# Expert tiles and shared rows fetched in column quarters and turned in 32x32 blocks on VectorE, with batched one-hots

## Chip, cores and metric

The kernel runs on one NeuronCore of a Trainium2 chip. The metric is the device time of one execution in microseconds (us). Below, PE is TensorE, DVE is VectorE, ACT is ScalarE, POOL is GpSimd, SP is SyncE.

## What is computed

A gated cross-attention block is followed by a gated mixture of experts, all in float32. x is (4, 512, 512), that is 2048 tokens of 512 features, and the context is of the same size.

```python
x = x + tanh(g_xattn) * xattn(layernorm(x), ctx)        # one head of 512, 512 + 512 keys
x = x + tanh(g_ffn) * moe(layernorm(x))

shared = silu(x @ W1s.T) * (x @ W3s.T) @ W2s.T          # hidden width 704
probs = softmax(x @ Wg.T)                               # 16 experts
topk_w, sel = top_k(probs, 4)
h = silu(einsum('td,efd->etf', x, W1)) * einsum('td,efd->etf', x, W3)   # hidden width 352
routed = einsum('etf,edf->td', h * combine.T[:, :, None], W2)
moe = shared + routed
```

## The kernel before

Four blocks follow each other, each with one instruction stream per engine and with semaphores between them; nothing reorders the instructions. Attention ends at about 434 us. The routing block (names with b_) runs to 552 us: PE computes the shared FFN for the first half of the tokens in two batches of 512, while DVE ranks the 16 probabilities of each token, counts the tokens of each expert and lists them. The expert block (c_) runs to 1051 us. The combining block (d_) computes the shared FFN for the second half of the tokens and adds up four expert rows for each token.

**Precision.** Each float32 operand is held as a high part (rounded to fp32r by ACT) and a low part (the difference, by DVE or POOL). Each product is three matmuls (line 86): high by high, low by high, high by low.

**The list.** 2048 tokens x 4 choices are 8192 slots, padded for each expert to tiles of 128. 128 x 64 one-hot rows (`one_hot`: line 1176 for the row in the tile, line 1177 for the tile) are multiplied by 64 matmuls (line 1286) into `slot_tokens`, the token of each slot. What DVE does between the steps of the shared FFN is in the table `work` of the routing block, whose key counts those steps: 6 of up and 4 of down for each batch.

**The expert block.** Here there are 72 tiles; 8 experts have five and 8 have four. A tile is 128 rows of 512 features, gathered by POOL with an indirect DMA into `xg[v]`, one of four buffers (v = t % 4), four tiles ahead. PE turns it with four transposes into PSUM (`c_ps_x`, line 1471), ACT copies the high part (line 1411) and DVE subtracts for the low one (line 1445). Up is 24 groups of three matmuls into `c_ps_u`, then silu on ACT, the product with it on DVE (`hf`, line 1459), three transposes (`c_ps_h`), high and low again, and down with 27 matmuls into `c_ps_y`. PE's order in step t is: turn(t), down(t - 2), turn_h(t - 1), up(t).

POOL's step t waits until tile t is gathered and turned, copies a column of the list, gathers tile t + 4, and at the first tile of an expert also does the weights: it waits for those of the next expert (`w_in`), computes their low part (`split_expert`, line 986, 128 x 3840 and 96 x 512 elements), waits for `y_ready`, and issues four DMAs for the weights of the expert after it (lines 977 and 978, twice 2.1 MB). At the last expert but one it issues the last down weights and `last_xs`, the first rows of the combining block, instead. SP only stores 16 tiles of zeros here. ACT stores each tile's result to DRAM (`y_dram`, 256 KB).

## Time and profile before

| | us |
|---|---|
| runs (three) | 1169.88, 1174.15, 1181.65; median 1174.15 |
| profiled execution | 1170.14, its span 1168.5 |
| PE busy | 1106.2 (95% of the span) |
| PE loading weights | 940.0 (80%) |
| DVE, ACT, POOL busy | 490.0 (42%), 279.6 (24%), 477.5 (41%) |
| mean granted clock of PE | 0.977 of full speed |

The busy time of an engine tells how much of the span it has instructions in execution; PE's matmuls overlap, so that the durations of single matmuls add up to more than the time they cost. In the timeline a row has a start in us from the start of the span, a duration, and the engine, line, operation and tiles (output <- input); in brackets is the idle time of the engine ahead of it and what ended it. "POOL idle L73" is a small instruction that stands where POOL waits for a semaphore. Times to landing run from the issue of a DMA to its last byte.

### The profile page before, as it was taken

The numbers are of one execution on the slowest core, as the hardware profiler recorded it, in microseconds if no ns is written. First come the engines' busy times: TensorE is split into PE (matmuls) and PEld (weight loads), VectorE is DVE, ScalarE is ACT, GpSimd is POOL, SyncE is SP. The second block draws the span as 40 slices with busy tenths as digits, with TensorE's granted clock in tenths as the row PEclk, the third lists the DMA queues.
The fourth block names the chain that finished last, engine by engine and source line by source line (L and its number), as shares of the span: only waits on it lengthen the run. The fifth ranks groups of instructions, "written<-read, shape, count | busy, mean of one in ns | idle before, by whom it ended". The sixth has DMA issues, their size and how long they took to land. (4 is left out here: it accounts for less than half of the span.)

```text
span 1168.5 us, 18611 instructions
## 1 busy us (share of the span) xinstructions
PE 1106.2 (95%) x5666; PEld 940.0 (80%) x5667; DVE 490.0 (42%) x994; ACT 279.6 (24%) x575; POOL 477.5 (41%) x521
## 2 busy tenths in 40 slices
PE   3999999999999959998989999999999999988997
PEld 3888878878878827686879999999999999977775
DVE  2243463445336255996222222222222222225847
ACT  1231131122113002111223333333333333321210
POOL 4720201201100235101665565556656665617763
PEclk9999999999999968899999999999999999998999
DMA  9411320312220528133864666666666666627785
GB/s 348 193 73 73 122 94 1 141 74 72 108 72 0 225 85 297 36 111 96 325 226 162 216 229 229 238 220 222 236 220 229 229 220 229 215 69 237 226 278 162
DMA packets 54209, 199.70 MB, mean 171 GB/s; under 512 B 7009, under 2 KB 7009, under 8 KB 45985
## 3 DMA queue, kind: packets, MB, share of 16 engines
q0 software_dynamic: 21184, 122.44, 30.1%
q1 hardware_dynamic: 22624, 57.98, 13.9%
q10 hardware_dynamic: 10368, 18.88, 4.3%
q8 instruction: 18, 0.29, 0.1%
q14 instruction: 15, 0.11, 0.0%
HBM read 161.51 MB, written 37.75 MB: 171 GB/s over the span
## 5 line engine op out<-in xcount | busy, mean ns | idle before, releaser
L86 PE MATMUL c_ps_u<-expert_hi,xT_hi 128*128 x576 | 192.7, 335 | 2.0 <-DVE xT_lo L1445 1.9
L86 PE MATMUL c_ps_u<-expert_hi,xT_lo 128*128 x576 | 186.0, 323 | 0.0
L86 PE MATMUL c_ps_u<-expert_lo,xT_hi 128*128 x576 | 185.6, 322 | 0.0
L986 POOL TENSOR_TENSOR expert_lo<-expert_raw,expert_hi (+3 forms) x39 | 158.2, 4079 | 19.9 <-issue 14.0
L73 POOL TENSOR_TENSOR idle<-idle 128x1 f32<-128x1 f32 x91 | 17.5, 192 | 232.0 <-PE c_ps_x L1471 141.3
L86 PEld LDWEIGHTS c_ps_u<-expert_hi,xT_hi 128*128 128x128 f32 x576 | 108.8, 189 | 2.9 <-issue 2.9
L86 PEld LDWEIGHTS c_ps_u<-expert_lo,xT_hi 128*128 128x128 f32 x576 | 109.3, 190 | 0.0
L1459 DVE TENSOR_TENSOR hf<-c_ps_u,gate 128x352 f32<-128x352 f32 x72 | 37.8, 525 | 170.3 <-ACT gate L1434 170.3
L86 PEld LDWEIGHTS c_ps_u<-expert_hi,xT_lo 128*128 128x128 f32 x576 | 108.7, 189 | 0.0
L1449 DVE TENSOR_TENSOR hT_lo<-c_ps_h,hT_hi 128x256 fp32r<-128x256 f32 x72 | 30.6, 425 | 181.4 <-ACT hT_hi L1424 181.4
L86 PE MATMUL c_ps_y<-expert_hi,hT_hi 128*128 (+1 forms) x216 | 91.7, 425 | 2.6 <-DVE hT_lo L1450 2.3
L86 PE MATMUL c_ps_y<-expert_hi,hT_lo 128*128 (+1 forms) x216 | 85.8, 397 | 0.0
L86 PE MATMUL c_ps_y<-expert_lo,hT_hi 128*128 (+1 forms) x216 | 85.6, 396 | 0.0
L1362 POOL DMA_INDIRECT xg<-xn_dram,column x72 | 71.4, 992 | 25.2 <-issue 19.9
L1596 POOL DMA_INDIRECT parts<-y_dram,token_slots x64 | 67.4, 1053 | 24.7 <-issue 19.2
L1434 ACT ACTIVATE gate<-c_ps_u 128x352 f32<-128x352 f32 x72 | 33.4, 464 | 181.4 <-PE c_ps_u L86 181.4
L1417 ACT ACTIVATE y<-c_ps_y 128x512 f32<-128x512 f32 x72 | 43.1, 598 | 113.0 <-PE c_ps_y L86 113.0
L417 DVE TENSOR_TENSOR q_lo<-ps_products,q_hi 128x512 fp32r<-128x512 f32 x32 | 22.1, 692 | 110.5 <-ACT q_hi L349 110.5
L292 POOL TENSOR_TENSOR ln_rstd<-ln_var,minus_half 128x4 f32<-128x4 f32 x8 | 8.2, 1028 | 145.3 <-DVE ln_var L430 145.3
L1623 DVE SCALAR_TENSOR_TENSOR total<-parts,combine_weights,total 128x512 f32<-128x512 f32 x64 | 54.2, 846 | 14.0 <-DMA total<-x_dram 8.3
L1445 DVE TENSOR_TENSOR xT_lo<-c_ps_x,xT_hi 128x512 fp32r<-128x512 f32 x72 | 49.8, 692 | 12.7 <-ACT xT_hi L1411 9.5
L349 ACT ACTIVATE q_hi<-ps_products 128x512 fp32r<-128x512 f32 x32 | 19.2, 598 | 149.4 <-PE ps_products L86 149.4
(268 smaller groups left out, 2454.5 us busy)
## 6 DMA issues: line engine op xcount, KB each, us to landing
expert_hi<-we POOLq DMA_DIRECT2D x16, 1920.0 KB, 7.9
expert_raw<-we POOLq DMA_DIRECT2D x14, 1920.0 KB, 13.0
y_dram<-y ACTq DMA_DIRECT2D x72, 256.0 KB, 2.1
ctxT_hi<-ctxT POOLq DMA_DIRECT2D x4, 1024.0 KB, 7.4
ctxT_raw<-ctxT SPq DMA_DIRECT2D x4, 1024.0 KB, 5.6
ctx_raw<-ctx SPq DMA_DIRECT2D x4, 1024.0 KB, 4.8
r_t<-x SPq DMA_DIRECT2D x4, 1024.0 KB, 5.3
ctx_hi<-ctx POOLq DMA_DIRECT2D x4, 1024.0 KB, 6.9
```

Source lines behind the costliest of these rows:

```text
L86: last = pe.matmul(out, a[i], b[j], start=(n == 0), stop=(n == 3 * len(pairs) - 1))
L349: act.activation(out, ps_m[:, (m.n - 1) % 2, :], ACT.Copy).then_inc(m_hi, 1)
L417: dve.tensor_tensor(lo, ps_m[:, (m.n - 1) % 2, :], hi, ALU.subtract).then_inc(m_free, 1)
L986: last = eng.tensor_tensor(lo, raw, hi, ALU.subtract)
L1362: pool.indirect_dma_start(xg[v][:], None, mem["xn2"], bass.IndirectOffsetOnAxis(ap=at, axis=0)).then_inc(gathered[v], 16)
L1417: act.activation(y[v][:], ps_y[:, v % 2, :], ACT.Copy).then_inc(y_taken, 1)
L1434: act.activation(gate[u][:], ps_u[:, u, 0, 0:FF], ACT.Silu).then_inc(gate_ready, 1)
L1445: dve.tensor_tensor(x[u][1][:], ps_x[:], x[u][0][:], ALU.subtract).then_inc(x_split, 1)
L1449: dve.tensor_tensor(h[u][1][:, 0:2, :], ps_h[:, 0:2, :], h[u][0][:, 0:2, :], ALU.subtract)
L1459: dve.tensor_tensor(hf[u][:], ps_u[:, u, 1, 0:FF], gate[u][:], ALU.mult).then_inc(h_ready, 1)
L1596: pool.indirect_dma_start(parts[v][:, q, :], None, y_d, bass.IndirectOffsetOnAxis(ap=keep["slots"][:, order[c], q:q + 1], axis=0)).then_in ...
L1623: ins = dve.scalar_tensor_tensor(out=total[k][:], in0=parts[c % 4][:, q, :], scalar=keep["weights"][:, order[c], q:q + 1], in1=total[k][:] ...
```

## The change

A tile of an expert no longer reaches PE in its gathered form. `xg[v]` is stored to a DRAM buffer (`bounce`) and loaded back in four DMAs, one for each quarter of the 512 columns, each to its own 32 partitions (`load_sides`); one DVE instruction turns the 32x32 blocks (`turn_sides`) into one buffer `xt`, from which ACT and DVE make the high and low parts. The rows of the up weights are permuted by the host to fit (`sides`). PE's transposes of tiles and `c_ps_x` are gone. The same is done with the rows of the shared FFN in the routing and combining blocks: each load of 128 rows becomes four, and eight times four transposes of PE in each block become eight of DVE. POOL's split of an expert's weights goes in pieces of 512 columns. The first four tiles are gathered by POOL at the routing block's end, and stored and loaded by ACT.

In the routing block the one-hots are built by six large instructions and 16 that multiply by the token (in place of 128 small ones), the counts come one step earlier in `work`, the schedule later, and the 64 matmuls of the list stand before the third up of the second batch instead of the last down. The second expert's weights are asked for when the schedule is made.

```diff
+def bounce(eng, mem, later, v):
+
+    return eng.dma_start(mem["bounce"][v * P:(v + 1) * P], later.xg[v][:])
+
+
+def load_sides(eng, rows, to, sem):
+
+    side = P // SIDE
+    part = rows.rearrange("(g i) (a c) -> a i g c", i=SIDE, a=side)
+    for a in range(side):
+        eng.dma_start(to[a * SIDE:(a + 1) * SIDE, :, :], part[a]).then_inc(sem, 16)
+
+
+def turn_sides(eng, out, rows):
+
+    return eng.transpose(out.rearrange("p k (g i) -> p g k i", i=SIDE), rows[:].rearrange("p g (k j) -> p g k j", j=SIDE))
 
...
+            def turn_about(t, v):
+                sp.wait_ge(x_turned, t - (QUAD - 1))
+                sp.wait_ge(gathered[v], (t + (QUAD - v)) * 4)
+                bounce(sp, mem, later, v).then_inc(bounced[v], 16)
+                sp.wait_ge(bounced[v], (t + (QUAD - v)) * 4)
+                load_sides(sp, mem["bounce"][v * P:(v + 1) * P], later.xs[v], loaded[v])
+
+            with sp.Fori(1, last + 1) as i:
+                for v in range(QUAD):
+                    turn_about(i * QUAD + v, v)
+            turn_about(last * QUAD + QUAD, 0)
...
             def step(t, v):
 
-                pool.wait_ge(gathered[v], (t + (QUAD - v)) * 4)
+                pool.wait_ge(bounced[v], (t + (QUAD - v)) * 4)
                 pool.tensor_copy(column[v][:], keep["index"][:, t + QUAD:t + QUAD + 1] if isinstance(t, int)
-                                 else keep["index"][:, bass.ds(t + QUAD, 1)]).then_inc(column_ready, 1)
-                pool.wait_ge(x_turned, t + 1)
-                pool.wait_ge(column_ready, t + 1)
+                                 else keep["index"][:, bass.ds(t + QUAD, 1)]).then_inc(pool_made, 1)
+                pool.wait_ge(pool_made, t + 2)
                 hold(nc, nc.gpsimd, keep)
                 gather(v, column[v][:])
                 flag = number(pool, t, "turn", 0, 2)
@@ -1382,7 +1440,7 @@
                     base = number(pool, t, "at1", 0, (BUFFERS - 1) * WE)
 
                     pool.wait_ge(w_in, e * 64 + 32)
-                    split_expert(pool, later, base, w_ready)
+                    split_expert(pool, later, base, w_ready, D)
...
-                            pool.dma_start(later.last_xs[i][:], xn2_d[2 * IT + i]).then_inc(keep["last_xs_in"][i], 16)
+                            load_sides(pool, xn2_d[2 * IT + i], later.last_xs[i], keep["last_xs_in"][i])
...
-            def turn(t, u):
+            def turn(t, v):
+                dve.wait_ge(loaded[v], (t + (QUAD - v)) * 16)
+                wait(dve, x_split, t)
+                turn_sides(dve, xt[:], xs[v]).then_inc(x_turned, 1)
+
+            def low(t, u):
                 dve.wait_ge(x_hi, t + 1)
-                dve.tensor_tensor(x[u][1][:], ps_x[:], x[u][0][:], ALU.subtract).then_inc(x_split, 1)
+                dve.tensor_tensor(x[u][1][:], xt[:], x[u][0][:], ALU.subtract).then_inc(x_split, 1)
 
             def turn_h(t, u):
                 dve.wait_ge(h_hi, t + 1)
@@ -1452,25 +1514,20 @@
 
             def step(t, v):
                 u = v % 2
-                turn(t, u)
+                turn(t + 1, (v + 1) % QUAD)
                 if later_than(t, 0):
                     turn_h(t - 1, 1 - u)
+                low(t + 1, 1 - u)
                 dve.wait_ge(gate_ready, t + 1)
                 dve.tensor_tensor(hf[u][:], ps_u[:, u, 1, 0:FF], gate[u][:], ALU.mult).then_inc(h_ready, 1)
 
+            turn(0, 0)
+            low(0, 0)
...
-            def turn(t, v):
-
-                pe.wait_ge(gathered[v], (t + (QUAD - v)) * 4)
-                wait(pe, x_split, t)
-                for k in range(DC):
-                    last = pe.transpose(ps_x[:, k, :], xg[v][:, k * P:(k + 1) * P], keep["ident"][:])
-                last.then_inc(x_turned, 1)
-
             def weights(base, start, n, rows=P):
...
+            def hot_rows(first, n):
+
+                i = slice(first, first + n)
+                dve.tensor_tensor(row_hot[:, i, :], lane[:].unsqueeze(1).broadcast_to([P, n, P]),
+                                  row_no[:, i].unsqueeze(2).broadcast_to([P, n, P]), ALU.is_equal).then_inc(hot_ready, 1)
+
+            def hot_tiles(k):
+
+                hot = tile_hot[k]
+                then(dve.tensor_tensor(hot[:], lane[:, 0:TILES_MAX].unsqueeze(1).broadcast_to([P, HN, TILES_MAX]),
+                                       tile_no[:, k * HN:(k + 1) * HN].unsqueeze(2).broadcast_to([P, HN, TILES_MAX]),
+                                       ALU.is_equal))
+                for j in range(HN // TOPK):
+                    at = k * HN // TOPK + j
+                    last = dve.tensor_scalar(hot[:, j * TOPK:(j + 1) * TOPK, :], hot[:, j * TOPK:(j + 1) * TOPK, :],
+                                             token[:, at:at + 1], None, ALU.mult)
                 last.then_inc(hot_ready, 1)
+
+            def weights():
...
-                    **{at: (lambda j=j: one_hot(j)) for j, at in enumerate(range(10, 17), 1)}}
+            def done():
+                then(dve.tensor_tensor(keep["turn"][:], t_f[:], t_g[:], ALU.mult))
+                dve.memset(t_f[:, 0:1], 0.0).then_inc(scheduled, 1)
+
+            piece = NT * TOPK // PIECES
+            work = {0: lambda: (rank(), choices()), 1: rest_of_down, 2: counts, 3: slots,
+                    4: lambda: hot_rows(0, piece), 5: lambda: hot_rows(piece, piece), 6: lambda: hot_rows(2 * piece, piece),
+                    7: lambda: hot_rows(3 * piece, piece), 8: lambda: hot_tiles(0), 9: lambda: hot_tiles(1),
+                    10: weights, 11: schedule, 13: lambda: places(range(BUFFERS)), 14: lambda: (turns(), done())}
 
             def between(n, k):
                 at = n * (SC + IT) + k
...
 
+                if n * (SC + IT) + j == LIST_AT:
+                    list_slots()
                 if (n, j) != (0, 3):
```

**SP in the expert block.** Before, SP has the stores of zeros and a wait for them. This is what stands behind them now, the first three tiles of its loop over four; `xg_69` to `xg_71` are gathered tiles, `xs_73` to `xs_75` what is loaded back, and `gathered`, `bounced` the semaphores of gather and store.

```order
L1323 DMA bounce_dram<-xg_69 128x512 [waits gathered0]
L1331 DMA xs_73<-bounce_dram 32x4x128 [waits bounced0]
L1331 DMA xs_73<-bounce_dram 32x4x128 x3
L1323 DMA bounce_dram<-xg_70 128x512 [waits gathered1,c_x_turned]
L1331 DMA xs_74<-bounce_dram 32x4x128 [waits bounced1]
L1331 DMA xs_74<-bounce_dram 32x4x128 x3
L1323 DMA bounce_dram<-xg_71 128x512 [waits gathered2,c_x_turned]
L1331 DMA xs_75<-bounce_dram 32x4x128 [waits bounced2]
L1331 DMA xs_75<-bounce_dram 32x4x128 x3
```

Each tile has a store that waits for its gather, and four loads that wait for the store; the next tile's store stands behind them in SP's row.

**POOL at a tile of the expert block, up to the wait ahead of the next weight loads.** Before:

```order
L1373 COPY column_3582<-slot_tokens 128x1 [waits gathered1]
L73 TENSOR_TENSOR idle<-idle 128x1 [waits c_column_ready,c_x_turned]
L1362 DMA xg_70<-xn_dram,column_3582 128x512
L986 TENSOR_TENSOR expert_lo<-expert_raw,expert_hi 128x3840
L986 TENSOR_TENSOR expert_lo<-expert_raw,expert_hi 96x512
L73 TENSOR_TENSOR idle<-idle 128x1 [waits c_y_ready]
```

The same place now:

```order
L1432 COPY column_3514<-slot_tokens 128x1 [waits bounced1]
L74 TENSOR_TENSOR idle<-idle 128x1 [waits c_pool_made]
L1421 DMA xg_70<-xn_dram,column_3514 128x512
L989 TENSOR_TENSOR expert_lo<-expert_raw,expert_hi 128x512
...
L989 TENSOR_TENSOR expert_lo<-expert_raw,expert_hi 128x256
L989 TENSOR_TENSOR expert_lo<-expert_raw,expert_hi 96x512
L74 TENSOR_TENSOR idle<-idle 128x1 [waits c_y_ready]
```

The column copy waits for the store of the tile in place of its gather, the wait for PE's transposes (`c_x_turned`) is gone, and the split is in nine pieces: seven of 512 columns on 128 partitions (the row that is shown, and six like it), one of 256 and one of 512 on 96.

**DVE, two steps of the expert block.** Before:

```order
L1445 TENSOR_TENSOR xT_lo_3566<-c_ps_x,xT_hi_3565 128x512 [waits c_x_hi]
L1449 TENSOR_TENSOR hT_lo_3576<-c_ps_h,hT_hi_3575 128x256 [waits c_h_hi]
L1450 TENSOR_TENSOR hT_lo_3576<-c_ps_h,hT_hi_3575 96x128
L1459 TENSOR_TENSOR hf_3571<-c_ps_u,gate_3569 128x352 [waits c_gate_ready]
L1445 TENSOR_TENSOR xT_lo_3568<-c_ps_x,xT_hi_3567 128x512 [waits c_x_hi]
L1449 TENSOR_TENSOR hT_lo_3574<-c_ps_h,hT_hi_3573 128x256 [waits c_h_hi]
L1450 TENSOR_TENSOR hT_lo_3574<-c_ps_h,hT_hi_3573 96x128
L1459 TENSOR_TENSOR hf_3572<-c_ps_u,gate_3570 128x352 [waits c_gate_ready]
```

Now:

```order
L1336 STREAM_TRANSPOSE xT<-xs_76 128x4x4x32 [waits c_x_split,tile_in3]
L1511 TENSOR_TENSOR hT_lo_3512<-c_ps_h,hT_hi_3511 128x256 [waits c_h_hi]
L1512 TENSOR_TENSOR hT_lo_3512<-c_ps_h,hT_hi_3511 96x128
L1507 TENSOR_TENSOR xT_lo_3500<-xT,xT_hi_3499 128x512 [waits c_x_hi]
L1522 TENSOR_TENSOR hf_3507<-c_ps_u,gate_3505 128x352 [waits c_gate_ready]
L1336 STREAM_TRANSPOSE xT<-xs_73 128x4x4x32 [waits c_x_split,tile_in0]
L1511 TENSOR_TENSOR hT_lo_3510<-c_ps_h,hT_hi_3509 128x256 [waits c_h_hi]
L1512 TENSOR_TENSOR hT_lo_3510<-c_ps_h,hT_hi_3509 96x128
L1507 TENSOR_TENSOR xT_lo_3498<-xT,xT_hi_3497 128x512 [waits c_x_hi]
L1522 TENSOR_TENSOR hf_3508<-c_ps_u,gate_3506 128x352 [waits c_gate_ready]
```

A transpose of the next tile stands at the head of each step, the subtract for the next tile comes behind the low part of h, and it reads `xT` from SBUF where it read `c_ps_x`.

## Rows read from the trace of the kernel before

**Rows 1.** Busy time of each engine, 600 to 1040 us; then clock, DMA share.

```profile
600.00:1040.00 440.00, 440.00 (x2631) 409.53 (x2630) 120.46 (x262) 143.78 (x330) 256.85 (x300) 1.00 0.61 215
```

**Rows 2.** The tile c_ps_x: who waited for it, us and times.

```profile
  POOL idle L73: 141.3, 37
```

**Rows 3.** Timeline of POOL in one expert: start, duration, instruction, [idle before].

```profile
733.69 0.60 POOL L977 DMA_DIRECT2D expert_hi<-we  x1
...
735.38 0.54 POOL L978 DMA_DIRECT2D expert_raw<-we_rest  x1
...
736.96 1.01 POOL L1362 DMA_INDIRECT xg<-xn_dram,column  x1 [0.50 <-issue]
...
755.50 0.98 POOL L1362 DMA_INDIRECT xg<-xn_dram,column  x1
...
757.30 9.73 POOL L986 TENSOR_TENSOR expert_lo<-expert_raw,expert_hi  x2 [0.82 <-issue]
...
767.13 0.60 POOL L977 DMA_DIRECT2D expert_hi<-we  x1
```

**Rows 4.** Timeline of POOL and PE, first three weight loads and a stop.

```profile
575.69 0.59 POOL L977 DMA_DIRECT2D expert_hi<-we  x1
...
591.90 0.78 PE L1471 MATMUL c_ps_x<-ident,xg 128*128 128x128 f32 x4 [4.63 <-DMA xg<-xn_dram,column]
...
604.80 0.60 POOL L977 DMA_DIRECT2D expert_hi<-we  x1
...
639.93 0.60 POOL L977 DMA_DIRECT2D expert_hi<-we  x1
```

**Rows 5.** Timeline of PE at one tile's transposes.

```profile
854.90 0.60 PE L1471 MATMUL c_ps_x<-ident,xg 128*128 128x128 f32 x4
855.26 0.48 PE L86 MATMUL c_ps_y<-expert_hi,hT_hi 128*128 x1
```

**Rows 6.** DMAs issued at 735-738, 725, 436, 1007: KB, us to landing.

```profile
expert_raw<-we_rest POOLq DMA_DIRECT2D x1, 192.0 KB, 13.5
xg<-xn_dram,column POOLq DMA_INDIRECT x1, 12.4
y_dram<-y ACTq DMA_DIRECT2D x1, 256.0 KB, 10.4
...
y_dram<-y ACTq DMA_DIRECT2D x1, 256.0 KB, 2.0
...
first_xs<-xn_dram SPq DMA_DIRECT2D x1, 256.0 KB, 2.7
...
xg<-xn_dram,column POOLq DMA_INDIRECT x1, 9.2
```

**Rows 7.** Timeline of DVE and SP: two subtracts, four DMA issues.

```profile
461.53 1.15 DVE L938 TENSOR_TENSOR b_h_lo<-b_h,b_h_hi 128x512 fp32r<-128x512 f32 x1
...
856.17 0.69 DVE L1445 TENSOR_TENSOR xT_lo<-c_ps_x,xT_hi 128x512 fp32r<-128x512 f32 x1
...
1051.14 1.80 SPq L1560 DMA_DIRECT2D total<-x_dram  x4
```

**Rows 8.** One line each: ns min/median/max, first and last start.

```profile
L986 POOL TENSOR_TENSOR expert_lo<-expert_raw,expert_hi x9: 976/1302/1736, 460.8 to 471.5; 128x512 fp32r<-128x512 f32 x7, 128x256 fp32r<-128x256 f32 x1, 96x512 fp32r<-96x512 f32 x1
...
L1002 POOL TENSOR_TENSOR last_down_lo<-last_down_raw,last_down_hi x5: 1285/1294/1309, 1073.6 to 1078.6; 128x512 fp32r<-128x512 f32 x5
...
L1623 DVE SCALAR_TENSOR_TENSOR total<-parts,combine_weights,total x64: 740/752/6853, 1065.2 to 1161.3; 128x512 f32<-128x512 f32 x64
...
L1177 DVE TENSOR_SCALAR tile_hot<-lane,tile_no,token x64: 315/321/329, 503.5 to 541.4; 128x80 f16<-128x80 f32 x64
```

**Rows 9.** Timeline of POOL and PE at tile 69.

```profile
1006.92 1.02 POOL L1362 DMA_INDIRECT xg<-xn_dram,column  x1 [0.50 <-issue]
...
1022.21 0.60 PE L1471 MATMUL c_ps_x<-ident,xg 128*128 128x128 f32 x4
```

**Rows 10.** Busy time of each engine, 480 to 486 us, columns as before.

```profile
480.00:486.00 6.00, 5.65 (x15) 3.62 (x15) 5.70 (x12) 2.17 (x4) 0.00 (x0) 0.50 0.00 0
```

More of the change, by code:

```diff
@@ L766 @@
 BUFFERS = 3
[L770 to L771 removed]
 HN = NT * TOPK // 2
+PIECES = 4
+LIST_AT = SC + IT + 2
 class Later:
@@ L786, in __init__ @@
         self.xg = [sb(f"xg{v}", [P, D], F32) for v in range(QUAD)]
+        self.xs = [sb(f"xs{v}", [P, P // SIDE, P], F32) for v in range(QUAD)]
         self.behind_xg = sb.at
@@ L795, in __init__ @@
         over = Sbuf(nc, self.second_hi)
-        last = over("first_xs3", [P, D], F32)
-        over.at = first_free + 4 * 4 * DC * D * 2
-        self.first_xs = [over(f"first_xs{i}", [P, D], F32) for i in range(IT - 1)] + [last]
+        sides = [P, P // SIDE, P]
+        last = over("first_xs3", sides, F32)
+        over.at = self.first_xs_at = first_free + 4 * 4 * DC * D * 2
+        self.first_xs = [over(f"first_xs{i}", sides, F32) for i in range(IT - 1)] + [last]
         self.behind_xs = over.at
@@ L809, in __init__ @@
         self.last_d_hi = over("last_down_hi", [P, SC, D], F32R)
-        xs = [over(f"last_xs{i}", [P, D], F32) for i in range(2)]
+        xs = [over(f"last_xs{i}", sides, F32) for i in range(2)]
         assert over.at <= self.second_hi + 4 * WE
@@ L814, in __init__ @@
         self.last_d_raw = low[1]("last_down_raw", [P, SC, D], F32)
-        self.last_xs = xs + [low[0](f"last_xs{i}", [P, D], F32) for i in range(2, 4)]
+        self.last_xs = xs + [low[0](f"last_xs{i}", sides, F32) for i in range(2, 4)]
         assert low[0].at <= self.second_lo + 4 * WE
@@ L882, in down @@
             tripled(pe, self.ps_y[:, i % 2, :], pairs, split).then_inc(self.y_ready, 1)
-        for i in range(IT):
-            turn(0, i)
         up_ready()
@@ L942, in vector @@
             turn(0, i)
+            if i:
+                split(0, i - 1)
+        split(0, IT - 1)
         for n in range(2):
@@ L966, in vector @@
                     turn(1, i + 2)
+                if n == 0 and i < IT - 1:
+                    split(1, i + 1)
                 between(n, SC + i)
@@ L1118, in _ @@
             sh.scalar(act)
+            for v in range(QUAD):
+                act.wait_ge(keep["gathered"][v], 16)
+                bounce(act, mem, later, v).then_inc(keep["bounced"][v], 16)
+            for v in range(QUAD):
+                act.wait_ge(keep["bounced"][v], 16)
+                load_sides(act, mem["bounce"][v * P:(v + 1) * P], later.xs[v], keep["loaded"][v])
         @block.vector
@@ L1154, in count, with choose, slots @@
                 keep["cum"] = cum
[L1156 to L1165 removed]
+            def choose(what, out):
+                for k in range(TOPK):
+                    then(dve.scalar_tensor_tensor(out=f["one"][:], in0=keep["ranks"][:], scalar=float(k),
+                                                  in1=what[:], op0=ALU.is_equal, op1=ALU.mult))
+                    then(dve.tensor_reduce(out[:, :, k], f["one"][:], AX.X, ALU.add))
+            def slots():
+                choose(f["slot"], slot_f)
                 then(dve.tensor_copy(keep["slots"][:], slot_f[:]))
@@ L1297, in expert_phase @@
         sb = Sbuf(nc, later.behind_xg)
-        xg, gathered = later.xg, keep["gathered"]
+        xg, xs = later.xg, later.xs
+        gathered, bounced, loaded = keep["gathered"], keep["bounced"], keep["loaded"]
+        xt = sb("xT", [P, DC, P], F32)
         x = [(sb(f"xT_hi{u}", [P, DC, P], F32R), sb(f"xT_lo{u}", [P, DC, P], F32R)) for u in range(2)]
+        y = [sb(f"y{v}", [P, D], F32) for v in range(QUAD)]
         gate = [sb(f"gate{u}", [P, FF], F32) for u in range(2)]
@@ L1654, in program @@
         keep["up_ready"], keep["first_ready"] = sem("up_ready"), sem("expert_split")
-        keep["first_xs_in"], keep["gathered"] = ([sem(f"{n}{i}") for i in range(4)] for n in ("first_xs_in", "gathered"))
+        keep["first_xs_in"], keep["gathered"], keep["bounced"], keep["loaded"] = (
+            [sem(f"{n}{i}") for i in range(4)] for n in ("first_xs_in", "gathered", "bounced", "tile_in"))
         keep["y_out"], keep["base_out"] = [sem(f"y_out{v}") for v in range(QUAD)], [sem(f"base_out{u}") for u in range(2)]
```

118 lines of the change are left out of this document (48 added, 70 removed).

## Prediction

> **What bounds the kernel now.** I read the busy time by stretch first, then the tiles of the expert block one engine at a time. From 600 to 1040 us PE is busy 440.0 of 440 us at full clock, while DVE and POOL have 27% and 58% of that stretch [rows 1]. What the change takes from PE there counts in full, as long as nothing else paces the tiles. The second reading asks how far off the others are. POOL is not idle for want of work: 141.3 us of its waits end with a c_ps_x transpose [rows 2], so it is held to PE's pace by the very instruction that goes. Its cycle for an expert of five tiles: weights asked for at 733.69, split begun at 757.30, next weights at 767.13 [rows 3]. That is 33.44 us, 6.69 for each tile of PE; an expert of four tiles takes 26.75. In the first expert, where PE was ahead of POOL, the same chain had PE idle for 4.63 us behind a gather [rows 4].
>
> **PE's transposes.** The first transpose of a tile starts at 854.90, the down matmul behind it at 855.26, and takes 0.48 us itself [rows 5]: 0.36, and my allowance of 0.06 for the slower start of another kind of matmul, 0.42 us a tile. The durations of the four overlap and don't add up to what PE gets back. 72 x 0.42 = 30 us if PE stays the bound; a five-tile expert would fall from 33.44 to 31.35 us, a four-tile one from 26.75 to 25.1.
>
> **The new path of a tile.** A tile is now gathered, stored to DRAM by SP, loaded back by four DMAs of SP, and turned on DVE. No row shows a DMA with 512-byte runs or a DVE transpose. For the store: 256 KB from SBUF landed after 2.0 us unloaded, and after 10.4 us when it was issued some 4 us after the weight loads [rows 6]. I take 2.3 where the weights have landed. For the load: 2.7 us for 256 KB in one piece [rows 6], bounds 2 and 5. SP's four loads of the combining block took 1.80 us to issue [rows 7], 0.45 each, so a tile holds SP for 0.15 + 2.3 + 4 x 0.45 = 4.3 us, below the 6.27 us of a tile: SP keeps up on the average. For the DVE transpose I take the 0.69 us that a 128x512 subtract needs [rows 7]; bounds 0.3 and 2. DVE's 27% becomes about 38%, so it is no bound by its busy time.
>
> The Trainium skill (DMA: Bandwidth & Descriptors, Rules for kernel authors) counts transfers under 64 KB as mostly overhead and asks to coalesce; four loads of 64 KB with 512-byte rows stand at its edge. The trace has no such load. By it the upper bound of 5 us would hold, and the sum below would be about 3 us higher in each place where a load is on the path.
>
> **The loop that will pace the experts.** POOL no longer waits for PE's transposes but for the store of the tile (`bounced`). Follow it from the first weight load of an expert, called L. The weights are in 15.2 us later (the last part issued at 735.38, 13.5 to landing); the gather behind them, issued 3.3 us after L, takes 12.4 us and lands at L + 15.7 [rows 3, 6]. In an expert of five tiles just this gather brings the tile at whose step the next split stands. So: 15.7 + 0.1 (wait) + 2.3 (store) + 0.1 + 2.06 (from the end of the last weight issue to that of the gather, 735.92 to 737.97) + 0.85 (from the gather at 755.50 + 0.98 to the split at 757.30, at most) + split + 0.15.
>
> The split was one piece of 3840 columns and one of 512, 9.73 us [rows 3]. It is now eight of 512 and one of 256, at 1.26 us for 512 (five took 6.29 [rows 8]): 8 x 1.26 + 0.65 = 10.7 us. DVE now has a subtract with both inputs in SBUF, turned beside these pieces; where such pieces ran beside such subtracts, in the routing block, a piece took up to 1.74 us and a subtract to 1.15 [rows 7, 8]. Two or three meet in one split: 11.5 us. The loop is 32.8 us, with 32.1 and 34 as its ends. Before: 33.44. **So of PE's 2.1 us a five-tile expert keeps 0.65.** A four-tile expert waits for its weights: 15.2 + 0.1 + 11.5 + 0.15 = 26.95, against 26.75 before: it loses 0.2.
>
> One thing more on SP. The gathers behind the weights land close together, and SP takes them 4.3 us apart. The fourth store is then issued at about L + 15.7 + 3 x 4.3 = L + 28.6. After a four-tile loop that is behind the next weight load, where a store takes 10 us and not 2; half of that is covered by the tiles ready ahead, and I count 1 us for each such loop.
>
> From 604.80 on there are six loops of five tiles and six of four. The first of five took 35.1 us [rows 4], and comes to 32.8 (-2.3); the other five give 5 x -0.65 = -3.2; the four-tile ones 6 x 0.2 = +1.2, and 6 x 1 = +6 for the late stores. Sum: +1.7.
>
> **The first expert.** L is at 575.69; the gather of tile 5 landed only at 591.9, and PE stood 4.63 us for it [rows 4]. Now PE would wait for store, load, transpose, high and low as well: 2.3 + 2.7 + 0.7 + 0.6 + 0.7, and it has 2 us less work in front. Only the tiles' end moves, and part of the next loop's slack takes it up: the next L was at 604.80; by the loop above it is 575.69 + 16.2 (the landing here) + 0.1 + 2.3 + 2.3 + 0.85 + 11.5 + 0.15 = 609.1. **+4.3.**
>
> **The end of the stage.** Behind the DMAs of the last weights and the four of last_xs, POOL issued the gather of tile 69 at 1006.92, with 9.2 us to landing [rows 6, 9]. It now stands behind 12 more issues, at 0.54 each as the one at 735.38 [rows 3] 6.6 us, and has store, load, transpose and split behind it, 7 us, before PE gets it. It landed at 1016.2 and was used at 1022.2 [rows 9], 6 us of slack. 6.6 + 7 - 6 = +7.6, less the part of these issues in which the queue has drained and the gather is quicker, 2 us: **+5**.
>
> **The other blocks.** In the routing block 32 PE transposes go (eight tiles, 8 x 0.4 = -3 us at most; four stand where PE waited anyway). The 128 one-hot instructions (64 of them of 0.32 us [rows 8]) become 4 + 2 large ones and 16 of 320 columns: by 0.69 us for 512 columns, 4 x 2.7 + 2 x 3.4 + 16 x 0.4 = 24 us, against some 27 as they overlap now. The counts move one place earlier; behind them PE stood before 480 us, and from 480 to 486 its clock was at 0.50 [rows 10]. That stall moves rather than goes. The list's 64 matmuls leave the end of the block; the gathers could come 5 us earlier, but they wait for the last up's release, the bounce adds 5 us, and the second expert's weights are asked for later. I take **-1** (bounds -5 and +4). In the combining block DVE does 8 more transposes and PE 32 fewer, and the start, where PE waits for DVE, is 0.7 us longer: **+1**. For the clock, one more stop of PE with such a stretch behind it, 6 us at 0.50 in which some 2 to 3 us of work are lost [rows 10]: **+2**.
>
> **The sum.** +1.7 + 4.3 + 5 - 1 + 1 + 2 = +13 us. The profiled execution took 1170.1 us, 4.0 below the median of the three runs, 1174.15; 1170.1 + 13 = 1183, and 1187 on the median's side. One per cent, 12 us, is about what a measurement of this kernel can tell from no change.
>
> **Rivals.**
> *PE stays the bound (0.15).* It needs a loop of 31.35 us: a gather landing 1 us sooner, a split of 10.7, no wait of DVE. For it: pieces of 512 may never meet a DVE subtract, as DVE has some 4 us of them in each 31. Then 66 x -0.42 = -28, with +5 at the start and +3 at the end: -20, 1154 us. Against: the landing at L + 15.7 is the trace's own, and the split can only grow.
> *It cancels (0.20).* Loops at the lower ends (-1.3 and -0.2 each) and no late stores: -9, start and end +8: 1165 to 1178, no difference to be told.
> *DVE is locked out by the split (0.20), the slower side.* In the combining block one DVE operation with two SBUF inputs stood 6.85 us, through five POOL pieces without a gap [rows 8]. If that is the rule for nine pieces, the subtract of the next tile stands 10.7 us, in front of hf and the transposed h that PE's down waits for. It decides from the point at which the lock lasts over one tile, 6.3 us: 4.4 us lost at each expert. 31.35 + 4.4 = 35.8 against 33.44, 25.1 + 4.4 = 29.5 against 26.75, so 16 x 2.5 = +40, and +7 for the ends: 1170 + 47 + 4 = 1221. Against: in the routing block subtracts got in between pieces after 1.15 us.
>
> The Trainium skill (SBUF — State Buffer, Who interferes with whom) says that GpSimd and a DVE instruction with two SBUF inputs lock each other out for a whole instruction. The 6.85 us row agrees and goes beyond it: five instructions, not one. By the page's rule a wait is at most one piece, 1.3 us, and the forecast stands.
>
> **Chances.** The forecast (+13, own range 1178 to 1200) has 0.45, in which a bit more than half lies over 1% slower. With the rivals: faster 0.18 (the first, and a little of the second), within 1% 0.37, slower 0.45. The range takes half of the first rival and half of the third: 1152 to 1222.
>
> **What the next profile would show.** Right: POOL's wait at the column copy ends with the store and not with PE; L to L is 32 to 34 us for five tiles and about 27 for four; PE idles 1 to 2 us in each expert, in c_ps_u behind DVE; PE's share falls below 92%; the gather of tile 69 is late by over 5 us. Wrong, if PE is busy all of 620 to 1000 (first rival), or if DVE's low stands over 5 us in each split (third). What would spoil it besides: 512-byte loads that take over 6 us, or a DVE transpose above 2 us.

## The result and the profile after

The change makes the kernel slower: 1260.34 us (median of four runs, 1257.52 to 1263.85) against 1175.48 us, a ratio of 1.0722 with a 95% interval of 1.066 to 1.0784. The forecast was 1187. The page of the changed kernel:

```profile
span 1256.4 us, 18614 instructions
PE 1095.5 (87%) x5314; PEld 919.9 (73%) x5315; DVE 544.0 (43%) x979; ACT 277.5 (22%) x576; POOL 516.1 (41%) x638
...
bounce_dram<-xg SPq DMA_DIRECT2D x69, 256.0 KB, 2.5
xs<-bounce_dram SPq DMA_DIRECT2D x276, 64.0 KB
```

PE is busy for 11 us less, in a span that is 88 us longer. The first column of the next table runs from the first to the last tile's h transposes (`c_ps_h`), that is the expert block without its edges; all are us.

| | expert block | before it | after it |
|---|---|---|---|
| before | 482.9 | 561.8 | 123.9 |
| changed | 555.1 | 572.7 | 128.5 |

72 us of the loss are in the expert block, 11 ahead of it, 5 behind it. Busy time of each engine in a stretch of the expert block, with the same columns as [rows 1]:

```profile
620.00:1040.00 420.00, 366.61 (x1984) 331.99 (x1984) 141.75 (x276) 117.72 (x276) 246.94 (x340) 0.94 0.75 261
```

PE, busy 100% of such a stretch before, is now idle for 53 us of 420, at a clock of 0.94. The waits of the block, engine by engine (us in total, times, longest; PE and DVE from 600 to 1110 us, POOL from 600 to 1040 us):

```profile
PE c_ps_y L87 <- DVE hT_lo L1512: 78.8, 16, 14.3
...
DVE xT L1336 <- DMA xs<-bounce_dram: 189.2, 37, 18.7
...
POOL column L1432 <- DMA bounce_dram<-xg: 75.7, 9, 11.9
POOL expert_lo L989 <- DMA expert_raw<-we_rest: 39.4, 6, 7.8
POOL idle L74 <- PE c_ps_y L87: 24.6, 10, 4.9
```

These lines are read as a chain. PE stops 16 times for the low part of h, at least once behind each request for weights; DVE has not made it because the turn of the next tile (the DVE transpose) stands ahead of it in DVE's queue; and the turn waits for the four loads of SP. One expert shows why, in the timelines of SP, POOL, DVE and PE (POOL's gap at 826.69 is what [rows 2] was):

```profile
800.07 0.34 SPq L1323 DMA_DIRECT2D bounce_dram<-xg  x1
802.76 1.73 SPq L1331 DMA_DIRECT2D xs<-bounce_dram  x4
804.65 0.34 SPq L1323 DMA_DIRECT2D bounce_dram<-xg  x1
806.76 1.91 SPq L1331 DMA_DIRECT2D xs<-bounce_dram  x4
823.55 0.34 SPq L1323 DMA_DIRECT2D bounce_dram<-xg  x1
826.55 1.73 SPq L1331 DMA_DIRECT2D xs<-bounce_dram  x4
828.39 0.36 SPq L1323 DMA_DIRECT2D bounce_dram<-xg  x1
...
806.40 0.61 POOL L980 DMA_DIRECT2D expert_hi<-we  x1 [1.17 <-issue]
...
826.69 0.19 POOL L1432 COPY column<-slot_tokens 128x1 int32 x1 [11.09 <-DMA bounce_dram<-xg]
...
829.37 11.66 POOL L989 TENSOR_TENSOR expert_lo<-expert_raw,expert_hi  x9 [0.97 <-issue]
...
843.17 0.61 POOL L980 DMA_DIRECT2D expert_hi<-we  x1 [1.07 <-issue]
...
824.07 0.71 DVE L1336 STREAM_TRANSPOSE xT<-xs 128x512 f32<-128x512 f32 x1 [7.62 <-DMA xs<-bounce_dram]
...
825.42 0.49 PE L87 MATMUL c_ps_y<-expert_hi,hT_hi 128*128 x1 [3.78 <-DVE hT_lo L1512]
```

The weights are asked for at 806.40. SP issues the loads of a tile 0.36 us later, and the turn behind them starts at 824.07, 17.7 us after the weights were asked for. That is when weights land: in the six loops where POOL's split waits for them, it starts 15.2 to 17.3 us after they were asked for. The gather issued at 809.45 took as long:

```profile
xg<-xn_dram,column POOLq DMA_INDIRECT x1, 14.0
```

It lands at 823.5, its store at 826.5, and that tile is turned at 830.16, 24 us after the weights were asked for. For 17 us SP starts on no tile; in the rest of the 36.8 us from one weight load to the next it passes four or five, at 4.0 to 5.9 us each, and the loads of the last one run into the next weights. The other experts are like this one: from SP's last DMA for a tile to its next there are 13 to 18 us at 13 of 14 weight loads, 9.5 at the other, and 14.8 in the median.

### The profile page after: what moved, and what is told of

Same layout as the page of the kernel before. It is cut to its first block and busy times, and to the rows that moved or that the text cites. A ratio compares the mean times of both kernels' runs of the same rounds, so it can differ in the third digit from the quotient of the medians.

```text
span 1256.4 us, 18614 instructions
## 1 busy us (share of the span) xinstructions
PE 1095.5 (87%) x5314; PEld 919.9 (73%) x5315; DVE 544.0 (43%) x979; ACT 277.5 (22%) x576; POOL 516.1 (41%) x638
## 5 line engine op out<-in xcount | busy, mean ns | idle before, releaser
L989 POOL TENSOR_TENSOR expert_lo<-expert_raw,expert_hi (+1 forms) x144 | 182.5, 1302 | 50.7 <-DMA expert_raw<-we_rest 40.8
L87 PE MATMUL c_ps_y<-expert_hi,hT_hi 128*128 (+1 forms) x216 | 95.7, 443 | 82.5 <-DVE hT_lo L1512 82.2
L1336 DVE STREAM_TRANSPOSE xT<-xs 128x512 f32<-128x512 f32 x73 | 51.7, 708 | 196.9 <-DMA xs<-bounce_dram 194.0
L87 PEld LDWEIGHTS c_ps_y<-expert_hi,hT_hi 128*128 128x128 f32 (+1 forms) x216 | 45.2, 209 | 95.9 <-issue 88.4
L87 PEld LDWEIGHTS c_ps_u<-expert_lo,xT_hi 128*128 128x128 f32 x576 | 110.6, 192 | 0.0
L87 PE MATMUL c_ps_y<-expert_lo,hT_hi 128*128 (+1 forms) x216 | 93.0, 431 | 0.0
L87 PE MATMUL c_ps_y<-expert_hi,hT_lo 128*128 (+1 forms) x216 | 92.9, 430 | 0.0
L1467 ACT ACTIVATE xT_hi<-xT 128x512 fp32r<-128x512 f32 x73 | 45.8, 628 | 142.3 <-DVE xT L1336 140.4
L1522 DVE TENSOR_TENSOR hf<-c_ps_u,gate 128x352 f32<-128x352 f32 x72 | 37.6, 522 | 85.9 <-ACT gate L1490 70.7
L74 POOL TENSOR_TENSOR idle<-idle 128x1 f32<-128x1 f32 x91 | 18.7, 206 | 128.1 <-PE ps_products L87 69.3
L1507 DVE TENSOR_TENSOR xT_lo<-xT,xT_hi 128x512 fp32r<-128x512 f32 x73 | 62.6, 858 | 5.8 <-ACT xT_hi L1467 5.7
```

What stands on the lines that cost most here:

```text
L74: return eng.tensor_tensor(idle[:, at:at + 1], idle[:, 4:5], idle[:, 4:5], ALU.add)
L87: last = pe.matmul(out, a[i], b[j], start=(n == 0), stop=(n == 3 * len(pairs) - 1))
L989: last = eng.tensor_tensor(lo, raw, hi, ALU.subtract)
L1336: return eng.transpose(out.rearrange("p k (g i) -> p g k i", i=SIDE), rows[:].rearrange("p g (k j) -> p g k j", j=SIDE))
L1467: act.activation(x[u][0][:], xt[:], ACT.Copy).then_inc(x_hi, 1)
L1507: dve.tensor_tensor(x[u][1][:], xt[:], x[u][0][:], ALU.subtract).then_inc(x_split, 1)
```

## The experiments

"Block" is the first column of the table above. Each time is that of one execution, but for the two at the end that have an interval (medians of ten and of twelve). The kernel before, measured beside these runs, took 1181, 1174, 1176, 1173 and 1174 us. Its executions scatter from 1169.84 to 1181.62 us (23 of them) and those of the changed kernel from 1257.52 to 1263.85 (four), so a difference of some 6 us between two single executions tells nothing.

**The expert block as before, the rest as changed.** PE turns the tiles, nothing is stored and loaded back, the split is in two pieces.

```diff
-  the expert block of the changed kernel; sides(w1), sides(w3)
+  the expert block of the kernel before; chunks(w1), chunks(w3)
```

> The expert block of the kernel before (four transposes of PE per tile, gathers used as they land, weights split in two pieces), with the routing and combining blocks of the changed kernel. If the new path of the expert tiles is the cause, the expert block has its 6.7 us a tile again, PE has one stop of some 5 us in it, and the time is 1180 to 1190 us, the routing and combining blocks keeping their +12. Rival, that the slower routing block also spoils the expert block (later second weights, later first tiles): over 1200 us.

1184.15 us, the block 482.4: the block is where it was before (482.9), so the whole of its loss is in its new path and none comes from a late routing block.

**Small weights.**

```diff
-    load_expert(pool, later.w_hi, ...); load_expert(pool, later.w_raw, ...)
+    pool.dma_start(part(w, P, base, 0, D), io["we"][e, :, 0:D])   # w_hi from the fourth expert on, w_raw from the third
```

> The changed kernel, but from the fourth expert on the weight loads carry 512 of 3840 columns (the split does the same work, on what is there), so that the traffic behind which tiles land is an eighth. The output is then not the reference's. If tiles stand behind the weights' transfer, PE's stops in the expert block go to under 1 us for each expert after the first two, and the time to 1165 to 1190 us. If DVE is locked out by POOL's pieces, or SP's serial store and loads are too slow by themselves, the stops stay and the time is above 1230 us.

1167.13 us, the block 464.5. The busy time of the stretch:

```profile
620.00:1040.00 420.00, 413.73 (x2363) 382.66 (x2361) 166.22 (x327) 139.72 (x329) 258.17 (x399) 1.00 0.66 200
```

With the same stores, loads, turns and POOL pieces, PE is idle for 6 us of 420 at full clock. The stops need the weights' transfer. The block is 18 us shorter than before, and 15 us of what is left are still stops: 9.5 us behind the weights of the third expert, whose high part is loaded whole, and 4.5 us near the block's end. Without any stop it would be near 450 us.

**Half the weights.**

```diff
-    load_expert(pool, later.w_raw, base, io, e, w_in)
+    pool.dma_start(part(later.w_raw, P, base, 0, D), io["we"][e, :, 0:D]) ...
```

> The changed kernel, but the raw part of an expert's weights is loaded only in its first 512 of 3840 columns (2.3 MB an expert in place of 4.2; the split does the same work; the output is not the reference's). The transfer then lasts some 9 us in place of 17. An expert of five tiles has 31 us for 9 + 5 x 4.6 = 32, one of four 25 for 9 + 18 = 27: stops of 1 to 2 us in each, 1180 to 1200 us. If the landing of the gather behind the weights were all, there would be none left (the gather lands 8 us earlier): below 1175 us.

1198.56 us, the block 495.6. A transfer half as long leaves a third of PE's waiting for h (28.4 us of 78.8, in 18 stops of at most 4.1 us); the time is at the upper end of what was expected.

**No store.**

```diff
-    bounce(sp, mem, later, v).then_inc(bounced[v], 16)
-    sp.wait_ge(bounced[v], (t + (QUAD - v)) * 4)
-    load_sides(sp, mem["bounce"][v * P:(v + 1) * P], ...)
+    load_sides(sp, mem["xn2"][v * P:(v + 1) * P], ...)
...
-    pool.wait_ge(bounced[v], (t + (QUAD - v)) * 4)     # POOL's step
+    pool.wait_ge(gathered[v], (t + (QUAD - v)) * 4)
```

> The changed kernel, but from the fifth tile on SP doesn't store the gathered tile; once it has landed, the four loads read fixed rows of the normalized input, and POOL goes on at the gather's landing (the tiles then hold other rows, and the output is not the reference's). A tile holds SP for 2 us in place of 4.6. If the time is 17 us of weights plus the tiles one by one, an expert needs 17 + 5 x 2 = 27 us, below PE's 31, and the stops all but go: 1175 to 1200 us. If the loads caught behind the weights stop PE by themselves, whatever the store, it stays above 1225 us.

1183.9 us, the block 484.8. The busy time of the stretch:

```profile
620.00:1040.00 420.00, 401.13 (x2267) 367.52 (x2266) 159.22 (x315) 134.50 (x315) 283.71 (x393) 0.99 0.76 261
```

PE is idle for 19 us of 420 where it was for 53. With 2 us of SP for a tile in place of 4.6 two thirds of the idle time go. The loads still meet the weights, and stops stay: 33.4 us in 12 of them from 600 to 1110 us, one of 12.2 us behind the weights of the third expert and the others of 0.8 to 3.4 us. So most of the loss takes both, a long transfer and a path of DMAs in series, each of which waits for the landing of the one before. The run doesn't part SP's time from POOL's earlier step, since POOL here goes on at the gather's landing.

**One load, or four of whole rows.** The first run loads a tile with one DMA, the second with four DMAs of 32 whole rows.

```diff
-    load_sides(sp, mem["bounce"][v * P:(v + 1) * P], later.xs[v], loaded[v])
+    sp.dma_start(later.xs[v][:], mem["bounce"][v * P:(v + 1) * P])                      # one load
+    for a in range(4): sp.dma_start(later.xs[v][32 a:32 a + 32], mem["bounce"][...])    # four of whole rows
```

> The changed kernel, but SP loads a tile back with one DMA of 256 KB in rows of 2 KB in place of four of 64 KB in rows of 512 bytes (features are then in the wrong order, and the output is not the reference's). If it is the weights' transfer that holds the tiles, whatever their form, the time stays within 1240 to 1262 us. If the four small loads are the cost (issue time, short rows), it falls below 1215 us.

> The changed kernel, but each of the four loads of a tile takes 32 whole rows of 2 KB in place of 128 pieces of 512 bytes (features in the wrong order, the output not the reference's). One load of 2-KB rows gave 1222 us. If the number of loads and their issue on SP made the 38 us, this run is at 1245 to 1262 us; if the 512-byte pieces made it, at 1215 to 1230 us.

1222.24 us with one (block 522.7), 1260.32 with four (554.5). The first result lay between the two expectations, so that the form of the load is a second cause: 38 us. The second shows which part of the form: 2-KB rows in place of 512-byte pieces gain nothing; what is left is that there are four DMAs and not one, with 1.73 us of issuing and not 0.35. SP's timeline with one load:

```profile
815.57 0.34 SPq L1323 DMA_DIRECT2D bounce_dram<-xg  x1
818.64 0.35 SPq L1408 DMA_DIRECT2D xs<-bounce_dram  x1
819.47 0.33 SPq L1323 DMA_DIRECT2D bounce_dram<-xg  x1
822.47 0.35 SPq L1408 DMA_DIRECT2D xs<-bounce_dram  x1
822.99 0.33 SPq L1323 DMA_DIRECT2D bounce_dram<-xg  x1
```

Here a tile takes 3.5 to 3.9 us in place of 4.0 to 5.9, so that more of them pass before the next weights.

**The raw weights behind one or two gathers.**

```diff
     gather(v, column[v][:])
+    load_raw(t - 1)          # t - 2 in the second run: the raw part of an expert asked for one step later
```

> The changed kernel, but the two weight loads of an expert are parted on POOL's queue: first the high part (2.1 MB), then the next tile's gather, then the raw part. The weights' transfer takes as long as before, but that gather stands behind 2 MB and not 4, and should land 8 to 9 us after the first weight load in place of 17. If it is this gather, with its store and load, that PE waits for, the stops shrink by some 4 us for each expert and the time falls to 1190 to 1225 us. If PE waits for the four loads of the tile before, which SP issued just as the weights started, and these are held until all weights are in, the stops stay: 1240 to 1262 us.

> As the run before, with two gathers between the high and the raw part of the weights, the raw part 3 to 4 us later. By the gather theory 1185 to 1220 us, no worse than with one gather, unless the weights' late landing delays the split: then the experts of four tiles grow to over 30 us, and the time is above the run before by 10 us or more.

1274.62 and 1242.22 us: the first is a clear miss for the gather theory and slower than either expectation had it, the second gains 18 us on the changed kernel, which neither of its expectations had. The DMAs of the first run tell why it lost; the first line is the loads of a tile ahead of the weights, the next two are loads and a gather issued 0.5 to 1.8 us behind the first weight load, the last is the store of the tile that this gather brought:

```profile
xs<-bounce_dram SPq DMA_DIRECT2D x4, 64.0 KB, 2.0
...
xs<-bounce_dram SPq DMA_DIRECT2D x4, 64.0 KB, 11.6
...
xg<-xn_dram,column POOLq DMA_INDIRECT x1, 8.8
...
bounce_dram<-xg SPq DMA_DIRECT2D x1, 256.0 KB, 9.3
```

The gather lands after 8.8 us, as foreseen, and nothing is won, since its store then runs beside the raw weights. The four loads landed after 8.7 to 16.9 us, and the turn needs the last of them. Whatever of a tile's three steps meets the weights takes some 9 us or more; to bring one step forward moved the meeting to the next. Why two gathers ahead of the raw weights did better than one was not looked into.

**Two tiles at a time on SP.**

```diff
+    for v in (v0, v0 + 1): wait for gather v; store v
+    for v in (v0, v0 + 1): wait for store v; four loads of v
```

> The changed kernel, but SP takes tiles in pairs: store, store, then the loads of the first and of the second, so that one store's landing is spent on the other's work. A pair should hold SP for some 6.7 us where two tiles held it for 9. If PE waits because SP can pass a tile only while no weights are in flight, and one at a time, an expert gets 4 to 5 us shorter where it stops now, as with the single load (1222 us): 1205 to 1235 us. If a tile's own latency through store and loads decides, the pair makes it worse: over 1255 us.

1255.14 us, where the account above asked for 1205 to 1235. It lies at the edge of the other branch (over 1255), but is not slower than the changed kernel as that branch had it; PE's waits for h are 78.8 us in both. The pair is quicker where both tiles are there, but not where the second is missing:

```profile
832.88 3.65 SPq L1331 DMA_DIRECT2D xs<-bounce_dram  x8
836.69 23.34 SPq L1323 DMA_DIRECT2D bounce_dram<-xg  x2
860.08 1.92 SPq L1331 DMA_DIRECT2D xs<-bounce_dram  x4
```

The first tile's store is issued at 836.69, the second's 23 us later, when its gather has come out from behind the weights, and the first tile's loads stand behind it. So the edit brought a wait of its own. That reading comes after a miss and no further run tests it; the run does not confirm the account above.

**The split: left out, and in two pieces.** In the first run POOL computes the last 96 x 512 only; in the second the pieces are those of before.

```diff
-    split_expert(pool, later, base, w_ready, D)
+    pool.tensor_tensor(lo, raw, hi, ALU.subtract)       # the last piece only; PE reads w_hi for w_lo
+    split_expert(pool, later, base, w_ready)            # second run: 3840 columns, and 512
```

> The changed kernel, but POOL computes the low part of the last 96 x 512 weights only, 1.3 us in place of 11.7, and PE multiplies by the high part where it took the low one (the output is not the reference's). If the tiles' landing behind the weights paces the block, PE's stops shrink only by what the next weight load comes earlier, and the time is 1235 to 1258 us. If the pieces lock out DVE, or POOL's time in them is what keeps the gathers late, it is below 1200 us.

> The changed kernel with the split in two pieces, 8.5 and 1.3 us, as before, in place of nine. The subtract of a tile, with both inputs in SBUF, then stands up to 8.5 us behind the long piece where it stood under 1.8 behind the short ones, but POOL is done 2 us sooner. If such a lock matters beside PE's long stops, the time is 1265 to 1300 us; if the stops hide it, 1250 to 1262 us.

1248.09 us without the split: DVE's lock by POOL (a DVE instruction that can't go on while POOL's runs) and POOL's time in the pieces together are worth 12 us of the 85. 1279.62 us in two pieces, 19 more than in nine. The subtract of the tile (min, median, max in ns), in the changed kernel and in this run:

```profile
L1507 DVE TENSOR_TENSOR xT_lo<-xT,xT_hi x73: 677/691/1781, 564.1 to 1123.8; 128x512 fp32r<-128x512 f32 x73
```

```profile
L1507 DVE TENSOR_TENSOR xT_lo<-xT,xT_hi x73: 677/678/7069, 560.6 to 1144.6; 128x512 fp32r<-128x512 f32 x73
```

The longest one of the second run stands in a long piece of POOL's; the row of POOL holds that piece, of 8.32 us, and the short one behind it:

```profile
604.96 10.00 POOL L989 TENSOR_TENSOR expert_lo<-expert_raw,expert_hi  x2 [1.02 <-issue]
606.76 7.07 DVE L1507 TENSOR_TENSOR xT_lo<-xT,xT_hi 128x512 fp32r<-128x512 f32 x1 [0.20 <-ACT xT_hi L1467]
```

The piece ends at 613.28 and the subtract at 613.83, in spite of the piece that follows. So the lock is real, it lasts for the piece that POOL is in, and the pieces of 512 columns keep it to 1.1 us (1.78 against 0.68).

**The low part of h ahead of the turn.**

```diff
-    turn(t + 1, ...); turn_h(t - 1, ...); low(t + 1, ...)
+    turn_h(t - 1, ...); turn(t + 1, ...); low(t + 1, ...)
```

> The changed kernel, but in each step DVE makes the low part of h first and then turns the next tile. In the changed kernel the turn heads the step, and while it waits for its loads, the low part of h stands behind it in DVE's queue, and PE's down (2.1 us) behind that: 82 us of PE's waits end with it. If what is queued behind the waiting turn is part of the loss, each of some 15 stops loses 2 us: 1225 to 1240 us, and the stops then lie ahead of the up matmuls. If the down only changes its place in the stop, because the next tile decides anyhow, 1250 to 1262 us.

1254.62 us: 70.6 us of PE's waits now stand ahead of the next h transposes. The order on DVE decides where PE stops, and hardly for how long (550.2 us in the block).

**The routing block.** The first run moves the counts alone back to where they were. The other three move slots and one-hot rows behind the last h of the first batch: once with the old expert block, once with the old expert block and the old turns of the shared rows, once in the changed kernel with the run before it.

```diff
-    2: counts, 3: slots, 4: hot_rows(0), 5: hot_rows(1), 6: hot_rows(2), 7: hot_rows(3)
+    3: counts, 4: slots and hot_rows(0), ...                                  # first run
+    3: counts, 5: slots, 6: hot_rows(0), hot_rows(1), 7: hot_rows(2), hot_rows(3)
```

> The changed kernel, but the counts of tokens stand one place later among DVE's work in the routing block, as before, with the slots behind them. If the earlier counts made the routing block's PE stop 3.6 us before the sixth up and 2.7 us before the first down, where it stopped 2.0 us before, the routing block shortens by 3 to 5 us and the time is 1252 to 1257 us. If the turns and the list's new place are the cause, it stays within 1 us of the changed kernel at the block's end.

> The run with the expert block of before (1184 us), in which moreover the counts stand at the place they had, and slots and one-hot rows behind the last h of the first batch (places 5 to 7 in place of 3 to 7). In the changed kernel 4.6 us of slots and 2.3 us of one-hot rows stand ahead of that h, and the first down began at 482.9 us in place of 474.8. If that order is the routing block's loss, this run begins it at 476 to 478, and takes 5 to 8 us less: 1176 to 1180 us, the same as before within 1%. If the turns on DVE are the loss there, it stays at 1184.

> The same, with the rows of the shared FFN loaded whole and turned by PE as before, so that of the change only the batched one-hots, their places and the list's new place are left. By the traces the turns cost 2.1 us at the start of the routing block and some 4 us in the combining block: 1170 to 1175 us, 0 to 0.5% below before. If the list and the one-hots cost time by themselves, it is above 1176.

> The same, with the counts, slots and one-hot rows at the places of the run d1. The routing block then begins its first down 5 to 7 us sooner: 5 to 8 us below the run before it.

| | first up to first down | first up to the end of the last down |
|---|---|---|
| before | 32.8 | 107.8 |
| changed | 38.8 | 113.4 |
| counts later (1257.67 us) | 33.1 | 113.6 |
| old experts (1184.15) | 38.6 | 111.6 |
| old experts, slots later (1178.98) | 33.1 | 110.6 |
| the same, old turns (1173.33) | 32.5 | 106.8 |
| h first (1254.62) | 39.0 | 113.6 |
| h first, slots later (1254.52) | 33.6 | 111.1 |

All are us, each read from one profiled execution. The counts alone give their gain back before the end. Slots and one-hot rows at their later places let the first down begin on time, but by the end only 1.0 us (old experts) or 2.5 us (h first) of the 5.6 are won. In the changed kernel 5 to 8 us in all were expected of them and nothing came: 1254.52 against 1254.62. Most of what is left goes with the turns: with the shared rows turned by PE the block is 3.8 us shorter, 1 us less than before. They cost 4 more ahead of the first up, 28.6 us from PE's first ps_transposed behind 410 us against 24.9. The ratios to the kernel before are 1.0034 (1.0012 to 1.0055) for the run with the turns and 1.0001 (0.9976 to 1.0027) for the one without. Batched one-hots and the list's new place alone change nothing that can be measured, and no variant that computes all of the output is faster than the kernel before.

## Why the prediction was wrong

**PE's transposes: right.** The h transposes of successive tiles, as they stand between two stops:

```profile
804.79 0.49 PE L1549 MATMUL c_ps_h<-ident,hf 128*128 128x128 f32 x3
811.02 0.49 PE L1549 MATMUL c_ps_h<-ident,hf 128*128 128x128 f32 x3
817.32 0.49 PE L1549 MATMUL c_ps_h<-ident,hf 128*128 128x128 f32 x3
```

6.23 and 6.30 us a tile, against 6.69, and 6.27 was predicted. PE's own work fell by the 30 us; stops and the clock took back more.

**The new path: the prices were right, "SP keeps up on the average" was the step that failed.** The turn takes 0.71 us (0.69 taken), four issues 1.73 us (1.80), a store 2.5 us in the median (2.3), with most between 2.1 and 3.7 once the weights are in. But 4.3 us for a tile were compared with 6.27 us of PE, as if SP could work all the time. It can't: for some 17 us after each weight load what it issues lands with the weights, and the next gather does too. As an estimate from the rows here, an expert of five tiles needs the 14.8 us in which SP is held and five tiles of 4.6, that is 38, where PE needs 31; from 623.55 us on the first weight loads of such experts are 34.6 to 40.5 us apart, 37.6 in the mean. Of four tiles it needs 33 by the same sum, and they are 27.5 to 34.2 apart, 31.2 in the mean, where PE needs 25: there the sum is 2 us too high. The late fourth store was seen, at L + 28.6 (L is the first weight load of an expert), and priced at 1 us for six loops. It is at L + 31.9 (838.26), and the tile behind it has its loads issued at 844.95, 1.8 us behind the next weight load; this meeting, or that of the store, comes with nearly every weight load and makes PE's stop. The 10.4 us row of [rows 6] held this: it was used for one store, and stands for every DMA on the path.

**The pacing loop: 32.8 us forecast, 36.8 here (806.40 to 843.17).** Its terms: the gather lands at L + 17.1 and not 15.7, the store 3.0 and not 2.3, the split 11.66 as estimated. These make 35. The rest stands behind the split: POOL waits 0.88 us for PE's down, which had itself stood for the loads, and 1.07 us more pass before the weight load, with no wait that the profile shows. From 600 to 1040 us such waits for PE come to 24.6 us in 10 loops: the loop runs through PE's stop, a path that the prediction did not follow.

**The clock: +2 forecast.** The whole block, with the columns of before:

```profile
572.70:1127.90 555.20, 474.77 (x2559) 429.72 (x2559) 182.47 (x355) 151.00 (x354) 317.67 (x442) 0.93 0.74 255
```

PE is idle for 80 us of it. It is busy for 475, where 71 tiles of 6.25 us need 444, and most of these 31 us are the clock: it was granted at 0.50, the lower of its two levels, in 12 stretches of 82 us together, in which PE was busy for 51 us; half of that, 25 us, is the estimate of what they cost. Each of these stretches begins within or just behind a stop of 2.4 us or more; the four stops of 0.4, 1.5, 2.5 and 3.1 us have none. They were not forecast since the stops were not.

**The other terms.** The first expert and the end of the stage were forecast to cost 9 us by the same path; they are inside the block's 72 and not measured apart. The routing block was forecast at -1, and it and the first tiles' store and loads cost 11: some 4 ahead of the first up, 5.6 in the block, 3 behind it, less 1.6 by which PE's part ahead of it began sooner. The step that failed is the price of the turns: they were to save up to 3 us, and DVE's time in them was put at nothing; the runs give them some 4 us ahead of the first up and 3.8 in the block. "That stall moves rather than goes" looked at the counts and not at the slots and the one-hot rows that came ahead of the last h too, 1.0 to 2.5 us. Combining: +1 forecast, 4.6 here; its first up begins 14.2 us behind the last h transposes in place of 12.0, and where the rest goes is open, as the run with the old turns has 128.1 us there too.

**The rivals.** None of them, nor the range, reaches 1260 us. Of the signs that were named, POOL's wait at the column copy ends with the store (75.7 us), and PE's share is under 92%; but PE's stops stand ahead of down and not of up, and are of 0.4 to 14.3 us, not 1 to 2. PE as the bound fell with the weights' transfer; it is what the run with small weights shows (1167 us, where 1154 was given to it). The lock-out of DVE had the right side, and 47 us of the 85, by a wrong cause: the longest subtract is 1.78 us, one piece and not nine. That a single instruction stood through five pieces in [rows 8] did not come back here: the same instruction takes 0.775 us at most in the changed kernel. The Trainium skill (SBUF — State Buffer, Who interferes with whom) has the lock for one whole instruction, and both runs agree: 1.78 us beside pieces of 1.29, 7.07 beside one of 8.32.

The other rule that was weighed (DMA: Bandwidth & Descriptors, Rules for kernel authors, of the Trainium skill: coalesce small transfers, under 64 KB they are mostly overhead) spoke against this change, whose loads are just at that size. The runs agree in part: four loads of 64 KB in place of one of 256 KB cost 38 us here, but with the one load the kernel still takes 1222 us, and the larger part of the loss is outside that rule.

## What to carry to other kernels

When a path gets more DMAs in series, ask what they take while the largest transfer of the loop is in flight, and count how many items pass in the time that is left, not in the whole loop. An engine that issues a DMA and waits for its landing before the next handles one item at a time, however idle it looks. And a step that leaves the critical engine is worth its time only if the tiles ahead of it last over the longest silence of the new path.

## What the runs showed of the hardware

Four loads of 64 KB on SP's queue that were issued 0.5 to 1.8 us behind a 2-MB load of POOL's queue, with 2 MB more issued at 4 us, took 8.7 to 16.9 us, 11.6 in the median, where those of the tile before took 2.0, though the queues are different ones. The length of the rows of the four loads, 512 bytes or 2 KB, made no difference (1260.34 and 1260.32 us); one load in place of four was 38 us quicker (one execution). The turn of 128x512 float32 in 32x32 blocks on DVE takes 0.71 us, about as much as a subtract of that size (0.69). A DVE subtract with both inputs in SBUF took up to 7.07 us beside a POOL subtract of 8.32 us and up to 1.78 us beside POOL's pieces of 1.3 us, where it took 0.68 by itself.
